# A Mamba-style decoder layer on one core: the state matmuls of a channel pair one slot later, ahead of the transposes, and a prologue shared out among engines

## The reference

```python
h = x * jax.lax.rsqrt(jnp.mean(x * x, axis=-1, keepdims=True) + EPS) * norm_w     # x is layer-normed before
proj = jnp.einsum('bsd,od->bso', h, in_proj_w)            # gate 8192 | hidden 8192 | B 1024 | C 1024 | dt 128
hBC = jax.nn.silu(causal_conv(hBC, conv_w, conv_b))       # 4 taps along the tokens
dt = jax.nn.softplus(dt + dt_bias);  A = -jnp.exp(A_log)
L = jnp.exp(segsum(Ac))                                   # decay between two tokens, per head, lower triangle
M = jnp.einsum('bcihn,bcjhn->bcijh', Ch, Bh) * jnp.transpose(L, (0, 2, 3, 4, 1))
Y_diag = jnp.einsum('bcijh,bcjhp->bcihp', M, hc)          # hc = hidden * dt
...
y = (Y_diag + Y_off).reshape(b, S, H_M, P_M)[:, :s] + D_res
yg = y * jax.nn.silu(gate)
ygr = ygr * jax.lax.rsqrt(jnp.mean(ygr * ygr, axis=-1, keepdims=True) + EPS)      # per group of 1024 channels
out = jnp.einsum('bsd,od->bso', y, out_proj_w);  return residual + out
```

## Time and profile before

| | us |
|---|---|
| median of 3 runs (lowest, highest) | 836.12 (833.25, 836.18) |
| profiled execution | 831.96 |
| its span | 830.2 |
| PE busy in the span | 791.9 (95%) |
| DVE, ACT, POOL busy | 621.9, 600.0, 623.6 |
| DMA, mean of the 16 engines | 114 GB/s |

### The profile page before, as it was taken

The page is one execution under the profiler, slowest core; times in us unless marked ns, Lnnn a source line. Parts: engine busy times, 40 slices in busy tenths (PEclk is TensorE's granted clock), DMA queues, the critical chain, the costliest instruction groups (busy, mean ns, idle before and its releaser), DMA issues.

```text
span 830.2 us, 13187 instructions
## 1 busy us (share of the span) xinstructions
PE 791.9 (95%) x4267; PEld 609.6 (73%) x4270; DVE 621.9 (75%) x752; ACT 600.0 (72%) x1047; POOL 623.6 (75%) x561
## 2 busy tenths in 40 slices
PE   6699899999999999999999999999999999989997
PEld 4566677777777777777777777777777777767664
DVE  7768878868677867778686876777786877788774
ACT  2578586888768777888678877888588876887442
POOL 6497774789857995789767986789677986786231
PEclk9889899999999999999999999999999999999999
DMA  7343232333143342433253333324243324330001
GB/s 283 128 152 120 72 128 90 128 128 127 64 156 126 124 127 94 145 103 128 67 185 127 96 120 135 124 93 155 79 159 123 119 78 153 128 125 29 3 2 51
DMA packets 48811, 94.92 MB, mean 114 GB/s; under 512 B 3952, under 2 KB 36848, under 8 KB 48784
## 3 DMA queue, kind: packets, MB, share of 16 engines
q1 hardware_dynamic: 48784, 94.58, 34.6%
HBM read 93.26 MB, written 1.31 MB: 114 GB/s over the span
## 4 chain that ended last, share of the span: by engine, by line
PE 60%; DVE 18%; ACT 11%; issue 8%; DMA 1%; POOL 1%; ACTq 0%; DVEq 0%; SPq 0%
PE ps_z L1075 18%; PE ps_out L1181 15%; PE ps_h L1075 12%; PE ps_y L1168 7%; DVE conv_bc L716 4%; ACT decay L519 4%; DVE conv L716 4%; PE ps_t L1053 2%; ACT L519 2%; ACT conv L467 2%; DVE yg L839 2%; DVE v L833 2%; ACT conv_bc L451 1%; DVE decay L774 1%; DVE y_lo L845 1%
## 5 line engine op out<-in xcount | busy, mean ns | idle before, releaser
L716 DVE SCALAR_TENSOR_TENSOR conv<-ps_h,w_raw,conv 128x510 f32<-128x510 f32 (+2 forms) x192 | 143.3, 746 | 102.1 <-ACT conv L467 97.5
L519 ACT ACTIVATE decay<-csx,cs_own 128x256 f32<-128x256 f32 (+1 forms) x512 | 184.4, 443 | 3.5 <-POOL csx L345 2.5
L307 POOL TENSOR_TENSOR win_lo<-w_raw,win_hi 128x1024 fp32r<-128x1024 f32 x64 | 153.0, 2391 | 0.0
L402 POOL TENSOR_TENSOR sqacc<-sqacc,sq 128x512 f32<-128x512 f32 x47 | 69.5, 1479 | 109.1 <-ACT sq L555 109.1
L774 DVE TENSOR_TENSOR decay<-decay,cbm 128x1536 f32<-128x1536 f32 x64 | 125.1, 1954 | 4.4 <-ACT decay L519 4.4
L527 ACT ACTIVATE hidT<-conv 128x512 f32<-128x512 f32 x64 | 40.5, 633 | 100.9 <-DVE conv L716 100.9
L1168 PE MATMUL ps_y<-decay,hid_dt 128*64 128x256 f32 (+1 forms) x1024 | 99.0, 336 | 12.4 <-DVE hid_dt L822 12.2
L1168 PEld LDWEIGHTS ps_y<-decay,hid_dt 128*64 128x64 f32 x1024 | 64.2, 138 | 55.7 <-issue 19.6
L345 POOL TENSOR_SCALAR_AFFINE_SELECT csx<-csx 128x512 f32<-128x512 f32 x128 | 103.8, 837 | 0.0
L1181 PE MATMUL ps_out<-wout_hi,y_lo 128*128 128x512 f32 x252 | 99.9, 397 | 0.0
L1181 PE MATMUL ps_out<-wout_lo,y_hi 128*128 128x512 f32 x252 | 99.5, 395 | 0.0
(11 more groups left out here) (315 smaller groups left out, 1490.5 us busy)
## 6 DMA issues: line engine op xcount, KB each, us to landing
w_raw<-in_wmain SPq DMA_DIRECT2D x64, 772.0 KB, 4.4
csx<-cs_rows SPq DMA_DIRECT2D x128, 256.0 KB, 3.5
bc_raw<-in_wbc SPq DMA_DIRECT2D x8, 517.0 KB, 3.6
ctx_raw<-in_ctx SPq DMA_DIRECT2D x1, 2048.0 KB, 14.2
acc<-in_x SPq DMA_DIRECT2D x4, 256.0 KB, 3.0
bc_raw<-in_wffn SPq DMA_DIRECT2D x2, 512.0 KB, 3.8
out_x<-acc SPq DMA_DIRECT2D x4, 256.0 KB, 2.1
csx<-in_wdt SPq DMA_DIRECT2D x1, 256.0 KB, 4.1
```

The costliest lines, as they stand in the source:

```text
L307: eng.tensor_tensor(win_lo[:, r2, :], w_raw[:, r4, 0:W_IN], win_hi[:, r2, :].bitcast(f32), ALU.subtract).then_inc(low_win, 1)
L402: eng.tensor_tensor(sqacc[:], sqacc[:], sq[:, (k - 1) % 2, :], ALU.add).then_inc(pool_sq, 1)
L519: done = eng.activation(decay[:, r2, b, h, lo:lo + n], csx[:, r2, b, h, lo:lo + n], ACT.Exp, bias=cs_own[:, r2, t, h:h + 1])
L716: eng.scalar_tensor_tensor(out=out_b[:, :, back:], in0=src_b[:, :, 0:S - back], scalar=w[:, TAPS - 1 - back:TAPS - back], in1=out_b[:, :, ...
```

## The change

1. Main loop. On PE the state matmuls of pair s-1 move from behind hidden(s) to the end of slot s, directly ahead of the transposes. In the slots `turned` (k = 0 and k = 7) the output matmuls stand ahead of gate(s). On DVE the masked product of pair s-1, the combination of pair s-2 and its `y_lo` now stand in slot s; the product of C and B is only copied to `cbm` (the causal mask is left out, since the decays above the diagonal are already zero). ACT makes decays(s) at the start of slot s in two halves, with `y_hi` and the square of pair s-2 between them.
2. Prologue. Half of x is loaded from ACT's queue; ACT makes two of the four normed tiles and two of the splits; `residual` is gone from DVE, POOL forms it with one operation per tile; softplus uses `ps_t` and `ps_out`; all four `w_raw` buffers are loaded at once, some FFN loads come in slot 4; 92 matmuls keep PE busy instead of 40.

```diff
 # SP
-                if not (first and k < 2):
+                if not (first and k < 4):
                     if late(s - 3):
                         eng.wait_ge(dve_ylo, s - 3)
                     eng.dma_start(w_raw[:, r, :], wmain_d[s]).then_inc(w_in[r], 16)
 # POOL, prologue and slot
             for t in range(TT):
-                eng.wait_ge(pre_dve, DVE_HT + t + 1)
-                eng.tensor_tensor(acc[:, t, :], acc[:, t, :], residual[t], ALU.add).then_inc(pre_pool, 1)
-            eng.wait_ge(pre_act, ACT_TOK)
+                eng.wait_ge(pre_dve, DVE_RES)
+                eng.wait_ge(pre_pe, KT)
+                eng.tensor_scalar(acc[:, t, :], acc[:, t, :], resid[:, 0, t:t + 1], resid[:, 1, t:t + 1], ALU.mult,
+                                  ALU.add).then_inc(pre_pool, 1)
+            eng.wait_ge(w_in[1], 16)
+            split_in(1, 1)
+            split_out(1)
+            lower_in(1, 1, 2)
+            lower_out(1, 2)
...
-                    if first and 0 < k < 3:
+                    if late(s):
                         eng.wait_ge(pe_gate, s)
                     if late(s - 2):
                         eng.wait_ge(pe_out, s - 2)
 # ACT, slot
+                decays(s, k, 0)
+                finish_y(s, g, k, first)
+                decays(s, k, 1)
...
                 tap(s, g, k)
-                hidden(s, k)
-                gates(s, k)
-                finish_y(s, g, k, first)
-                if not (last and k == PPG - 1):
-                    decays(s + 1, k + 1)
...
+                hidden(s, k)
+                gates(s, k)
 # DVE, prologue and slot
-            for t in range(TT):
-                pre(eng.tensor_scalar(residual[t], acc[:, t, :], mv[:, t, 0:1], rstd[:, t:t + 1],
-                                      ALU.subtract, ALU.mult))
...
             def slot(eng, s, g, k, first, last):
-                r2 = k % 2
+                if not (first and k < 2):
+                    combine(s, k)
                 if not (first and k == 0):
                     scale_hidden(s, k)
                 if k == 2 and not first:
                     add_group(g - 1)
+                if not (first and k == 0):
+                    mask(s, g, k)
+                if not (first and k < 2):
+                    lower_y(s, k)
...
-                if not (first and k == 0):
-                    combine(s, k)
-
-                eng.wait_ge(act_exp, s + 1)
-                eng.tensor_tensor(decay[:, r2], decay[:, r2], cbm[:].unsqueeze(2).broadcast_to([P, B, 2, MJ]),
-                                  ALU.mult).then_inc(dve_m, 1)
-                if not (first and k == 0):
-                    lower_y(s, k)
...
+            def mask(s, g, k):
+                eng.wait_ge(act_exp, s)
+                if k == 1:
+                    eng.wait_ge(dve_cb, 2 * g + 2)
+                q2 = (k - 1) % 2
+                eng.tensor_tensor(decay[:, q2], decay[:, q2], cbm[:].unsqueeze(2).broadcast_to([P, B, 2, MJ]),
+                                  ALU.mult).then_inc(dve_m, 1)
...
             def combine(s, k):
-                eng.wait_ge(pe_y, s)
-                eng.wait_ge(act_hid, s)
+                eng.wait_ge(pe_y, s - 1)
+                eng.wait_ge(act_hid, s - 1)
...
             def lower_y(s, k):
-                eng.wait_ge(act_yhi, s)
+                eng.wait_ge(act_yhi, s - 1)
 # PE, slot
+                turned = k == 0 or k == PPG - 1 and not last
                 project(ps_h[:], win_hi[:, r2, 0:KT * P], win_lo[:, r2, 0:KT * P], pe_hid)
-                if not (first and k == 0):
-                    scan_heads(s, k)
...
+                if turned and not (first and k == 0):
+                    project_out(s, g, k)
...
                     project(ps_z[:], win_hi[:, r2, KT * P:], win_lo[:, r2, KT * P:], pe_gate)
-                if not (first and k < 2):
-                    project_out(s, g, k)
+                if not turned and not (first and k < 2):
+                    project_out(s, g, k)
+                if k == 0:
+                    products_of_bc(s, g)
+                if k == 1 and not first:
+                    sum_channels(s, g - 1)
+                if not (first and k == 0):
+                    scan_heads(s, k)
                 eng.wait_ge(act_hid, s + 1)
                 ...
             def project_out(s, g, k):
                 eng.wait_ge(dve_ylo, s - 1)
```

More of the change, by code:

```diff
@@ L89, in build @@
         ident = sb("ident", [P, P])
-        causal = sb("causal", [P, MJ])
         ones = sb("ones", [P, 1])
@@ L215, in _ @@
         def _(eng):
-            for t in range(TT):
+            for t in range(0, TT, 2):
                 eng.dma_start(acc[:, t, :], x_d[t // 2, (t % 2) * P:(t % 2 + 1) * P, :]).then_inc(x_in[t], 16)
@@ L298, in split_in @@
                 eng.tensor_scalar(win_hi[:, r2, :], w_raw[:, r4, 0:W_IN], 1.0, 0.0, ALU.mult,
[L299 removed]
+                                  ALU.add).then_inc(hi_win, 1)
             def split_out(r4):
@@ L357, in slot @@
                 n4 = (k + 1) % 4
+                if first and k == 0:
+                    own_sums(1, 1)
+                    eng.wait_ge(csx_in[1], 32)
+                    select(1)
+                    return
+                if k == 2 and not first:
+                    eng.wait_ge(dve_ms, g)
+                    eng.tensor_tensor(rstd[:], ms[:], half_neg[:], ALU.pow).then_inc(pool_rstd, 1)
                 if not (last and k == PPG - 1):
                     eng.wait_ge(w_in[n4], 16 * (2 * g + (k + 1) // 4 + 1))
-                    if first and 0 < k < 3:
+                    if late(s):
                         eng.wait_ge(pe_gate, s)
@@ L431, in _ @@
         def _(eng):
+            for t in range(1, TT, 2):
+                eng.dma_start(acc[:, t, :], x_d[t // 2, (t % 2) * P:(t % 2 + 1) * P, :]).then_inc(x_in[t], 16)
             eng.wait_ge(wdt_in, 16)
             eng.activation(wdt_hi, wdt, ACT.Copy).then_inc(pre_act, 1)
+            eng.wait_ge(bc_in, 16)
+            eng.activation(wbc_hi[:], bc_raw[:, 0:BC_W], ACT.Copy).then_inc(hi_wbc, 1)
+            for t in range(1, TT, 2):
+                eng.wait_ge(pre_dve, DVE_NMR)
+                eng.activation(normed[:, t, :], acc[:, t, :], ACT.Identity, bias=resid[:, 2, t:t + 1],
+                               scale=lnr[:, 0, t:t + 1]).then_inc(pre_act, 1)
+            eng.wait_ge(w_in[0], 16)
+            eng.activation(win_hi[:, 0, :], w_raw[:, 0, 0:W_IN], ACT.Copy).then_inc(hi_win, 1)
             eng.wait_ge(pre_in, 32)
@@ L507, in slot, with decays @@
                     scale_context(PPG - 1)
-            def decays(s, k):
-                r2 = k % 2
-                eng.wait_ge(pool_own, s + 1)
-                eng.wait_ge(pool_sel, 2 * s + 2)
-                if late(s - 1):
-                    eng.wait_ge(pe_y, s - 1)
-                for b in range(B):
+                if k == PPG - 1 and not last:
+                    silu_bc(0, g + 1, conv_bc[:])
+                if k == 0:
+                    silu_bc(1, g, conv_bc[:])
+                hidden(s, k)
+                gates(s, k)
+            def decays(s, k, part=None):
+                r2 = k % 2
+                if part != 1:
+                    eng.wait_ge(pool_own, s + 1)
+                    eng.wait_ge(pool_sel, 2 * s + 2)
+                    if late(s - 1):
+                        eng.wait_ge(pe_y, s - 1)
+                for b in range(B) if part is None else (part,):
                     for h in range(2):
@@ L520, in decays @@
                                                   ACT.Exp, bias=cs_own[:, r2, t, h:h + 1])
-                done.then_inc(act_exp, 1)
+                if part != 0:
+                    done.then_inc(act_exp, 1)
             def hidden(s, k):
@@ L664, in _ @@
                 pre(eng.bn_stats(stats[:, t, :], acc[:, t, :]))
-            for t in range(TT):
-                eng.wait_ge(pre_dve, t + 1)
+                eng.wait_ge(pre_dve, n_pre[0])
                 pre(eng.bn_aggr(mv[:, t, :], stats[:, t, :]))
@@ L747, in slot @@
                     add_group(g - 1)
+                if not (first and k == 0):
+                    mask(s, g, k)
+                if not (first and k < 2):
+                    lower_y(s, k)
                 if k == PPG - 1 and not last:
                     conv_group(0, g + 1, ps_z, conv_bc[:])
-                if k == 0:
-                    conv_group(1, g, *((ps_y, gate[:, 1, :]) if first else (ps_z, conv_bc[:])))
-                if first and k == 0:
-                    conv_hidden(s, k)
+                if k == 0 and not first:
+                    conv_group(1, g, ps_z, conv_bc[:])
+                conv_hidden(s, k)
+                if k == 0 and first:
+                    conv_group(1, g, ps_y, gate[:, 1, :])
                 if k == 0:
@@ L1058, in keep_up @@
                     mm(bank[:, 0:P], identb[:], identb[:], start=True, stop=True)
-            eng.wait_ge(pre_pool, 9)
-            keep_up(ps_t, WARM_UP)
```

(15 more changed lines are left out.)

267 lines of the change are left out of this document (134 added, 133 removed).

## The result

The changed kernel took 875.62 us (median of 4 runs, 867.25 to 885.74) against 835.16 for the kernel before: ratio 1.041 (95% interval 1.037 to 1.045), slower. On another chip, later, it took 879.14 against 833.66, ratio 1.055 (1.051 to 1.059). The forecast was 855, range 811 to 873. Two executions, one of them the profiled one, had a lower granted clock (0.983 and 0.986; the others 0.992), and the ratio 1.041 is from the others, 867.25 to 870.71. These lie in the range, at its upper end; the median of all four and the 879.14 of the other chip lie above it. The execution profiled took 885.74, span 883.9, against 831.96 and 830.2 before; 53.7 us of span are to be explained.

The account below looks back on a forecast made before the run. PE was taken to bound the kernel. Loop gains -22.1, `y_lo` waits +53.9, prologue -9.1 and end +1.0 gave +23.7 us on the profiled 831.96, or 855.7; the forecast said 855, range 811 to 873.

Parts of the forecast that it names:

- waits for `hid_dt` and bcT, slow PE behind 94 us: Main loop: later state matmuls remove waits of 12.2 and 1.5 us, and 2.2 of slower PE behind a 3.37 wait.
- transitions: PE, main loop: state matmuls to gate(s) no longer occurs, gaining 0.10 in each of 62 slots, 6.2 us.
- waits for `y_lo`: PE before output matmuls: `y_lo`, now made in its own slot, comes late; 7.15 us a group, +53.9 in all.
- prologue: Before the loop: shorter DVE path and earlier weight split, against more ACT work; -9.1 us, bounds -5 and -13.
- end: Behind the last slot: two combinations instead of one, and last state matmuls wait for `hid_dt`; +1.0 us, bounds 0 and 2.
- L: Time when `y_lo` is done on DVE; 4.67 us after the previous slot's state matmuls end, if undisturbed.
- E: End of the state matmuls of slot s-1 on PE; PE reaches slot s's output matmuls 5.95 us later.
- rival D: PE, main loop: new step from state matmuls to transposes eats the 6.2 us gain; 861, inside the range.
- rival C: Worse: PE runs slower behind waits, 2.2 us once a group, plus the longer order everywhere; 878, chance 0.08.
- the longer order everywhere: `win_lo` ahead of the masked product, PE waiting 1.35 us; in every slot, the upper bound of 8.3 a group.
- A: Main loop: POOL's `win_lo` falls behind the masked product in most slots, only k = 2 waits; 812, chance 0.22.
- B: Main loop: POOL, late behind k = 4, stays late into the next group, only k = 0 to 2 wait; 834, chance 0.10.

Follow-up runs that it names:

- run 3: Changed kernel with one added wait: POOL starts `win_lo` only once the masked product is done; 845.62 us, ratio 1.015.
- run 4: Changed kernel with `win_lo` computed for only 512 of 1024 columns from slot 2 on, which changes the result; 860.53 us, ratio 1.030.
- 6: Changed kernel with `win_lo` for 512 of 1024 columns from slot 2 on, and `add_group` last on DVE at k = 2; 833.86 us, ratio 1.001.
- run 12: Changed kernel, PE order kept: POOL's `win_lo` waits for the masked product every slot, squares earlier at k = 1, `y_lo` before `add_group` at k = 2; 822.74 us.
- run 10: Changed kernel: output behind state matmuls (k = 1 to 6), `add_group` last at k = 2, squares earlier at k = 1, `win_lo` waits at k = 0; 813.84 us.
- run 2: Changed kernel with `y_lo` moved on DVE ahead of `add_group` and the masked product; 871.97 us, ratio 1.045.
- 7: Changed kernel with the output matmuls behind the state matmuls in slots k = 1 to 6, on PE alone; 852.16 us, ratio 1.023.
- 8: Changed kernel with output matmuls behind state matmuls in k = 1 to 6, and `add_group` last on DVE at k = 2; 852.12 us, ratio 1.019.

## Why the prediction held, point by point

The sign and the mechanism held; of the sizes, the waits for `y_lo` were too small and two terms that cost something stood at nothing. The last column is by steps of PE, which is the measure that the forecast used: the time from one start of the transposes to the next, less what such a slot takes without any wait. A wait costs more by steps than its row says: 0.16, as the matmul ahead of it is modelled to its end, and mostly 0.10 more in the steps behind it (the 12 output matmuls take 2.97 to 3.00 up to the state matmuls, without a wait 2.89).

| term | forecast | in the profile after |
|---|---|---|
| waits for `hid_dt` and bcT, slow PE behind 94 us | -15.9 | -16.8 (by rows 11.4 + 1.5, slow PE 2.7, the rest by steps) |
| transitions | -6.2 | -5.7 |
| waits for `y_lo` | +53.9 | +72.0 (58.8 by rows) |
| prologue | -9.1 | -7.1 (the transposes ahead of slot 2 begin at 45.47, not 52.53) |
| clock behind waits | 0 | +7.8 (five places) |
| sum of squares at k = 1 | 0 | +2.5 |
| end | +1.0 | +1.0 |

The measured terms add up to the 53.7; the waits for `y_lo` are what the others leave of the slots' sum.

**What held.** *"If PE waits for L ... POOL starts right at E"*: it does (360.17 for E = 360.12), and *"`win_lo` ... gets in ahead of the masked product"* is so at k = 1, 3 and 4. The signs came: 41 waits, longest 2.1, few at k = 6 and 7 (one each), slot 1 at 34.35, yg 0.80 and `y_lo` 1.11 in the rows above. Experiments 3, 4 and 6 show the cause by taking it away: with `win_lo` behind the masked product the waits for `y_lo` fall from 58.8 to 9.2, with half of it to 32.0, and with `add_group` behind `y_lo` as well to 9.8, at the time of the kernel before.

**The term that was too small: the waits for `y_lo`.** The group of the rows above waits 1.85, 1.03, 1.71, 1.13, 1.43 for k = 0 to 4 and not at 5 to 7, in sum 7.15, and the forecast was 1.25, 1.4, 1.85, 1.15, 1.15 and 0.35, in sum 7.15 too. That is luck, for I had worked out when `y_lo` ends less when PE gets there, which is a step. By steps the group waits 2.03, 1.19, 1.87, 1.29, 1.60 and 0.20, which is 8.2, and 0.8 more in the steps behind the waits: 9.0, above even my upper bound of 8.3. Most of the difference is at k = 0 and k = 4. In the profile this term alone is 18 us above the forecast.

**The transitions, rival D.** The sum is right and the way to it isn't. I took 0.10 from each of 62 slots for want of a row. In an ordinary slot nearly all of it comes back, as the rival had it: transposes to hidden(s) takes 0.41 instead of 0.35 and output to state matmuls 2.89 instead of 2.81, hidden(s) 2.86 instead of 2.95 and gate(s) 2.80 instead of 2.89. So a slot without a wait is 10.42 on average (10.43 from 394.74 on, for one), and was 10.45. The gain lies at k = 0, where the C times B products now follow the gate projection: 14.47 instead of 14.91; at k = 1 it is 11.20 instead of 11.36. (In the profile after, PE waits in every slot of k = 0 and 1; these two are run 12's, which has the same order on PE.) A slot of run 10 is 10.44, so in an ordinary slot PE's order by itself decides next to nothing.

**The prologue.** PE begins slot 1 8.05 us earlier, as forecast, but then waits 2.0 for `hidT` ahead of the next transposes, which it didn't before; 7.1 are left.

**The clock, rival C.** I had argued from one wait of 3.37 and expected no wait above 2, so none of this. The clock fell behind waits of 1.85 to 1.92 already, for 1.55 each and not 2.2, and not each time. I gave the rival the longer order everywhere as well, which did not come; C in its smaller form belonged into the sum. In run 4 it nearly doubled the price of the wait at k = 2. The 2.2 were themselves too small: by steps PE lost 2.7 behind the wait at 94 us.

**k = 0.** The forecast was 1.25; 1.85 came by the row, 2.03 by steps. There POOL is earlier, as I had said, and `win_lo` falls on yg, which takes 2.60, not on the masked product:

```profile
319.48 2.60 DVE L866 TENSOR_TENSOR yg<-v,gate 128x512 f32<-128x512 f32 x1
```

```profile
319.12 2.41 POOL L297 TENSOR_TENSOR win_lo<-w_raw,win_hi 128x1024 fp32r<-128x1024 f32 x1
```

**Rivals A and B.** Neither came. At k = 0 and 2 the waits repeated from group to group within 0.1 us but for the last group; at k = 1 and 4 they went from 1.0 to 2.1, and one group had none at k = 1. A was given 0.22 with the words that phases rest on differences of 0.1. That PE's own wait sets when the weights land, and so holds the phases, fits the rows (`y_lo` ends at 355.52, the load is issued at 355.70, POOL starts at 360.17); no run tests it by itself.

On the rule of the Trainium skill ("SBUF — State Buffer", "Who interferes with whom"), by which who issues first has the shared port for its whole instruction: the trace of run 10 agrees, in the row of `y_lo` above, 2.95 instead of 0.75 with `win_lo` (2.41) issued 0.01 ahead; and the wait that made the kernel faster, run 3, is a use of that rule.

## What to carry to other kernels

Before an engine's work is moved towards a nearer deadline, add up the whole chain up to it, with what the other engines do at that very time, since the move itself sets when the loads land. A wait added to the engine with time to spare can keep it out of the way of one that has none (22 us in run 3, 10 in run 10). And when one wait is taken away, look in each slot at who was just in time: in run 2 the next ones in line took all of the gain, in runs 3, 7 and 8 a good part of it. When a forecast and a profile are compared, compare the same measure: a wait's row was 0.26 short of what the wait cost.
